# Fuse weights read from PSUM, low weights moved to GpSimd, and a new order in the tail of a transformer and convolution kernel

## What is computed

```
xn = layernorm(x);  x = x + window_attention(xn)        # 8x8 windows, 8 heads, relative bias
x  = x + gelu(layernorm(x) @ w_mlp1) @ w_mlp2           # hidden 256
h  = pw1_w x + pw1_b                                    # pointwise, 64 -> 64
scores = sigmoid(fc2(relu(fc1(mean(h)))));  mask = the top 32 channels of each image
h  = relu(h);  offsets = tanh(mean(h) @ off_w + off_b)  # (B, 3, 2)
for i, (ksz, base) in ((3, dw3), (5, dw5), (7, dw7)):
    w = base[:32] * (1 + sigmoid(offsets[:, i, 0])) + tanh(offsets[:, i, 1])   # per image
    y_i = depthwise_conv((h * mask)[:, :32], w)
out = pw_w[:, :96] @ concat(y_3, y_5, y_7) + pw_b + x
```

## Time and profile before

| what | us |
|---|---|
| median of 3 runs | 320.33 |
| lowest and highest of them | 318.23, 321.41 |
| the profiled execution's own time | 316.19 |
| its span, first to last instruction | 314.3 |
| busy: TensorE, weight loads | 269.3, 212.8 |
| busy: VectorE, ScalarE, GpSimd | 231.6, 204.7, 154.4 |
| mean granted TensorE clock | 0.965 |

### The profile page before, as it was taken

How to read it: one execution, slowest core, us unless ns; L and a number is a source line. 1 busy time by engine, 2 the same in 40 slices (tenths; PEclk the granted TensorE clock), 3 DMA queues, 4 the chain that set the end, 5 groups by cost and what they waited for, 6 DMA issues and landing times.

```text
span 314.3 us, 6646 instructions
## 1 busy us (share of the span) xinstructions
PE 269.3 (86%) x2486; PEld 212.8 (68%) x2486; DVE 231.6 (74%) x450; ACT 204.7 (65%) x331; POOL 154.4 (49%) x193
## 2 busy tenths in 40 slices
PE   1566869899999999999989799968995999799992
PEld 1334656777767677776868546644495999699992
DVE  2867527488787887878878554898799999998222
ACT  6686743858669595776745889976541764898800
POOL 5053444667678676875751707094577000444400
PEclk9996998999999999999989999997999799999998
DMA  7981357335334343443530000741306765699841
GB/s 163 200 170 46 76 129 159 82 84 111 88 81 98 85 86 73 100 103 74 114 93 3 2 0 2 161 95 28 89 12 121 154 148 103 151 185 190 180 80 33
DMA packets 35118, 31.06 MB, mean 99 GB/s; under 512 B 20816, under 2 KB 30032, under 8 KB 35088
## 3 DMA queue, kind: packets, MB, share of 16 engines
q1 hardware_dynamic: 30608, 23.55, 32.5%
q0 software_dynamic: 3392, 6.17, 11.2%
q10 hardware_dynamic: 1088, 0.94, 1.5%
HBM read 4.54 MB, written 2.10 MB: 21 GB/s over the span
## 4 chain that ended last, share of the span: by engine, by line
PE 34%; DVE 23%; POOL 19%; issue 11%; SPq 5%; ACT 4%; DMA 3%; DVEq 0%; POOLq 0%; ACTq 0%
PE psum L1256 11%; POOL parts L334 8%; PE psum L1001 5%; POOL k_blocks L551 5%; POOL q_blocks L559 4%; PE psum L1157 3%; SPq L446 3%; PE psum L922 2%; PE psum L1061 2%; DMA k_heads<-k_parts 2%; PE psum L1020 2%; PE psum L975 2%; DVE conv_w L334 2%; DVE whole_w L1624 2%; SPq L458 2%
## 5 line engine op out<-in xcount | busy, mean ns | idle before, releaser
L1256 PE MATMUL psum<-shifted,conv_w 128*128 128x286 f32 x528 | 73.2, 299 | 2.0 <-ACT conv_w L849 1.8
L1256 PEld LDWEIGHTS psum<-shifted,conv_w 128*128 128x128 f32 x528 | 71.3, 192 | 3.5 <-issue 3.5
L1001 PE MATMUL psum<-q_heads,k_blocks 128*128 128x256 f32 x384 | 63.3, 304 | 2.8 <-ACT probs L707 2.2
L1001 PEld LDWEIGHTS psum<-q_heads,k_blocks 128*128 128x128 f32 x384 | 52.4, 194 | 13.8 <-ACT probs L707 6.3
L1406 DVE TENSOR_REDUCE maxima<-psum 128x8 f32<-128x512 f32 x64 | 40.5, 680 | 7.2 <-PE psum L975 7.2
L707 ACT ACTIVATE probs<-psum 128x512 f32<-128x512 f32 x64 | 37.6, 605 | 11.6 <-PE psum L1001 10.5
L551 POOL DMA_DIRECT2D k_blocks<-k_parts x56 | 32.2, 582 | 8.6 <-PE psum L1001 8.6
L334 POOL TENSOR_TENSOR conv_w<-whole_w,conv_w 128x1408 fp32r<-128x1408 f32 x4 | 12.9, 3226 | 40.8 <-ACT conv_w L843 40.8
L334 POOL TENSOR_TENSOR parts<-x,parts 128x256 fp32r<-128x256 f32 (+1 forms) x21 | 19.3, 930 | 27.7 <-ACT parts L656 20.0
L922 PE MATMUL psum<-parts,center_average 128*128 128x512 f32 x64 | 23.9, 457 | 9.7 <-DVE parts L334 7.9
L334 POOL TENSOR_TENSOR parts<-square_logvar,parts 128x512 fp32r<-128x512 f32 x13 | 19.2, 1480 | 26.1 <-ACT square_logvar L720 15.8
(11 more groups left out here) (154 smaller groups left out, 509.9 us busy)
## 6 DMA issues: line engine op xcount, KB each, us to landing
shifted<-images SPq DMA_DIRECT2D x32, 243.8 KB, 4.5
q_heads<-q_parts SPq DMA_DIRECT2D x128, 32.0 KB, 2.3
k_blocks<-k_parts POOLq DMA_DIRECT2D x56, 64.0 KB
k_heads<-k_parts SPq DMA_DIRECT2D x64, 32.0 KB, 2.2
out<-x SPq DMA_DIRECT2D x8, 256.0 KB, 3.3
q_blocks<-q_parts POOLq DMA_DIRECT2D x28, 64.0 KB, 2.4
conv_w<-conv_w SPq DMA_DIRECT2D x10, 176.0 KB, 3.6
x<-in_x SPq DMA_DIRECT2D x6, 256.0 KB, 5.1
```

Source lines behind the costliest of these rows:

```text
L1001: ins = pe.matmul(bank[:, hh * G // 2:(hh + 1) * G // 2], k_blocks[:, hh, w // (NW // 2), k_part, w % (NW // 2), :], q_heads[:, w // (NW / ...
L1256: ins = pe.matmul(psum[:, CONV[bh][g], 0:SPAN], conv_w[bh][:, w_part, h * NSLOT + slot, :], shifted[:, bh, part, stream, first:first + SPA ...
```

## The change

- `fuse_w` is copied once into a PSUM bank (`fuse_bank`) between the high and low parts of the last group's second layer norm, and `factors` reads it from there for all units; `whole_weights_by_banks` is otherwise as it was.
- GpSimd computes the low weights of units 2 and 3 too; VectorE's `low_weights(1, 0)` and `(1, 1)` are gone. `whole_weights_by_banks` now always waits for the low weights of unit u - 2.
- All pointwise products from group 2 on use one bank and wait for the ReLU of the group before. The MLP's result goes to bank 7 for groups 3 to 6; two hidden blocks of group 1 use two banks freed by the layer norm. The order of the first MLP products changes.
- ScalarE: `gelu(7)` ahead of `even_high(0)`, `relu(7)` (the last) ahead of `even_high(1)`, and gate 2 behind all moves of unit 2's high part.
- TensorE: gate 1's steps and gate 2's `gate_means` and `gate_scores` stand later.
- VectorE: each `add_mlp` from 4 on stands one place earlier, `gate_means(2)` ahead of the products of unit 2, `gate_spread(2)` ahead of the additions of unit 3 but behind its products.

```diff
@@ -259,7 +259,7 @@
             "gate_dve", "gate_pe", "gate_act", "dv_product", "dv_whole", "po_no_row", "ac_high", "ac_odd", "ac_odd_high", "low_weights", "dv_odd",
             "shift_in0", "shift_in1", "pe_conv", "dv_result", "out_done")}
 
-        HIDDEN0, MLP, PW1, GATE = 3, 1, (7, 2), 0
+        HIDDEN0, MLP, PW1, GATE = 3, 1, 2, 0
         CONV = ((3, 4, 5), (2, 6, 7))
 
         def x_view(g, s):
@@ -292,12 +292,12 @@
         fuse_bank = psum[:, MLP, 320:512].rearrange("p (m c) -> p m c", c=C)
         product5_banks = psum[:, GATE:MLP + 1, 0:320].rearrange("p h (s c) -> p h s c", c=C)
 
-        def factors(b4, bh, m, fuse=fuse_w):
+        def factors(b4, bh, m):
 
             shape = [128, NKT // TAP, KERNELS[m], C]
             tap = tap_w[:, m, bass.ds(2 * b4 + bh, 1), :]
             tap = tap.rearrange("p b (h x) -> p (b h) x", x=TAP)[:, :, TAP - KERNELS[m]:]
-            return tap.unsqueeze(3).to_broadcast(shape), fuse[:, m, :].unsqueeze(1).unsqueeze(1).to_broadcast(shape)
+            return tap.unsqueeze(3).to_broadcast(shape), fuse_bank[:, m, :].unsqueeze(1).unsqueeze(1).to_broadcast(shape)
 
         ODD_ROWS = ((64, 0, 64, 0, 0, NTILE), (32, 64, 32, 0, 0, NTILE), (0, 96, 32, NSLOT, 0, NSLOT))
 
@@ -310,16 +310,19 @@
         MEANS = 48
 
         def pointwise_bank(n):
-            return GATE if n < 2 else PW1[1 - n % 2]
+            return GATE if n < 2 else PW1
+
+        def hidden_bank(n, m):
+            return (MLP, NORM)[m] if n == 1 and m < 2 else HIDDEN0 + m
 
         def norm2_bank(c):
             return PV if isinstance(c, int) and c == NG - 1 else NORM
 
         def means_bank(k):
-            return MLP if k == 2 else GATE
+            return PV if k == 2 else GATE
 
         def mlp_bank(n):
-            return MLP if n < NG - 1 else HIDDEN0 + 2
+            return MLP if n < 3 else PV if n < NG - 1 else HIDDEN0 + 2
 
         MAX_BANKS = (MAX0, MAX0 + 1, MISC1)
 
@@ -628,7 +631,7 @@
             for n in range(5, NG):
                 low_image(n, n // 2, n % 2)
 
-            for u in range(4, B):
+            for u in range(2, B):
                 bh = u % 2
                 pool.wait_ge(S["ac_high"], u + 1)
                 low_part(pool, whole_w[:, bh].rearrange("p h t c -> p (h t) c"), conv_w[bh][:, 0, :, 0:C], conv_w[bh][:, 1, :, 0:C]).then_inc(S["low_weights"], 1)
@@ -811,7 +814,7 @@
             def gelu(n, par, blocks=range(4)):
                 for m in blocks:
                     act.wait_ge(S["pe_mlp1"], 4 * n + m + 1)
-                    act.activation(hidden[:, par, m, :], psum[:, HIDDEN0 + m, :], ACT.Gelu,
+                    act.activation(hidden[:, par, m, :], psum[:, hidden_bank(n, m), :], ACT.Gelu,
                                    bias=mlp1_bias[:, m % 2:m % 2 + 1]).then_inc(S["ac_gelu"], 1)
 
             def relu(n, b4, half):
@@ -842,13 +845,12 @@
                     act.wait_ge(S["pe_conv"], u - 1)
                 act.copy(conv_w[bh][:, 0, :, 0:C], whole_w[:, bh].rearrange("p h t c -> p (h t) c")).then_inc(S["ac_high"], 1)
 
-            def odd_high(u, bh, moves=range(3), done=True):
+            def odd_high(u, bh, moves=range(3)):
                 act.wait_ge(S["ac_high"], u + 1)
                 for m in moves:
                     to, of = odd_rows(bh, 0, m)
                     ins = act.copy(to, of.bitcast(F32))
-                if done:
-                    ins.then_inc(S["ac_odd_high"], 1)
+                ins.then_inc(S["ac_odd_high"], 1)
 
             def odd_low(u, bh):
                 act.wait_ge(S["low_weights"], u + 1)
@@ -889,20 +891,19 @@
             relu(3, 1, 1)
             gelu(6, 0)
             relu(4, 2, 0)
+            gelu(7, 1)
             even_high(0, 0)
+            relu(5, 2, 1)
             odd_high(0, 0, range(1))
-            gelu(7, 1)
             gate(1)
-            relu(5, 2, 1)
             relu(6, 3, 0)
+            relu(7, 3, 1)
             even_high(1, 1)
             odd_high(1, 1, range(1))
-            relu(7, 3, 1)
             keep_shared(0, 0)
             even_high(2, 0)
-            odd_high(2, 0, range(1), done=False)
+            odd_high(2, 0)
             gate(2)
-            odd_high(2, 0, range(1, 3))
             odd_low(2, 0)
             keep_shared(1, 1)
             high_weights(3, 1)
@@ -1054,11 +1055,15 @@
                 pe.wait_ge(S["dv_normed2"], 2 * n + 2)
                 for m in blocks:
                     bh, f = m // 2, m % 2
-                    if n > 0:
+                    if n == 1 and m == 0:
+                        pe.wait_ge(S["ac_log2"], NG - 1)
+                    elif n == 1 and m == 1:
+                        pe.wait_ge(S["dv_whole2"], NG - 1)
+                    elif n > 0:
                         pe.wait_ge(S["ac_gelu"], 4 * n + m - 3)
 
                     for part in range(2):
-                        ins = pe.matmul(psum[:, HIDDEN0 + m, :], mlp1_w[:, part, f * 128:(f + 1) * 128],
+                        ins = pe.matmul(psum[:, hidden_bank(n, m), :], mlp1_w[:, part, f * 128:(f + 1) * 128],
                                         normed2[:, bh, bass.ds(n * G, G)], start=part == 0, stop=part == 1)
                     ins.then_inc(S["pe_mlp1"], 1)
 
@@ -1145,7 +1150,10 @@
 
 
             def mlp2(n, par):
-                pe.wait_ge(S["ac_log2"], NG - 1)
+                if n == 0:
+                    pe.wait_ge(S["ac_gelu"], 5)
+                if n == 3:
+                    pe.wait_ge(S["dv_whole2"], NG)
                 if n == NG - 1:
                     pe.wait_ge(S["ac_gelu"], 4 * NG)
                 elif n > 0:
@@ -1162,15 +1170,13 @@
 
                 pe.wait_ge(S["dv_x2"], n + 1)
                 if n == 0:
-                    pe.wait_ge(S["dv_whole2"], NG - 1)
+                    pe.wait_ge(S["ac_gelu"], 6)
                 if n == 1:
                     pe.wait_ge(S["ac_relu"], 1)
                 if n == 2:
                     pe.wait_ge(S["ac_log2"], NG)
-                if n == 3:
-                    pe.wait_ge(S["dv_whole2"], NG)
-                if n > 3:
-                    pe.wait_ge(S["ac_relu"], n - 1)
+                if n > 2:
+                    pe.wait_ge(S["ac_relu"], n)
                 pixels = x2[:, bass.ds(n * G, G)].rearrange("p (y v k q) -> p q v y k", v=2, q=2, k=W // 2)
                 for q in range(2):
                     ins = pe.matmul(psum[:, pointwise_bank(n), q * G // 2:(q + 1) * G // 2], pw1_w, pixels[:, q], start=True, stop=True)
@@ -1210,14 +1216,15 @@
                 pe.matmul(psum[:, GATE, 0:n], mem["score_rep"][0:n], consts[0:n, a:a + n], start=True, stop=True).then_inc(S["gate_pe"], 1)
 
             mlp1(0, range(2, 4))
+            mlp1(1, range(0, 2))
             projection(NG - 1)
-            mlp1(1, range(0, 2))
+            mlp1(1, range(2, 4))
             mlp2(0, 0)
-            mlp1(1, range(2, 4))
+            mlp1(2, range(0, 2))
             pointwise1(0, 0)
             centered2(NG - 1)
             mlp2(1, 1)
-            mlp1(2)
+            mlp1(2, range(2, 4))
             pointwise1(1, 1)
             variance2(NG - 1)
             mlp1(3)
@@ -1238,12 +1245,12 @@
             pointwise1(4, 0)
             mlp2(5, 1)
             mlp1(7)
-            gate_means(1)
             pointwise1(5, 1)
             mlp2(6, 0)
+            gate_means(1)
+            mlp2(7, 1)
             gate_scores(1)
             pointwise1(6, 0)
-            mlp2(7, 1)
 
 
             def passes(bh, w_part, g):
@@ -1297,13 +1304,13 @@
             low_passes(0, 0)
             high_weights_in(0, 1)
             passes(1, 0, 0)
+            passes(1, 0, 1)
             gate_means(2)
-            passes(1, 0, 1)
-            gate_scores(2)
             passes(1, 0, 2)
             low_passes(0, 1)
+            gate_scores(2)
+            high_passes(1, 0)
             gate_spread(2)
-            high_passes(1, 0)
             low_passes(1, 0)
             high_passes(1, 1)
             low_passes(1, 1)
@@ -1621,6 +1628,7 @@
 
 
             def products(b4, bh):
+                dve.wait_ge(S["dv_fuse"], 1)
                 dve.tensor_tensor(taps_window(whole_w[:, bh], 2), *factors(b4, bh, 2), ALU.mult)
                 dve.tensor_tensor(product5[:], *factors(b4, bh, 1), ALU.mult)
                 dve.tensor_tensor(product3[:], *factors(b4, bh, 0), ALU.mult).then_inc(S["dv_product"], 1)
@@ -1649,11 +1657,10 @@
 
             def whole_weights_by_banks(b4, bh):
                 u = 2 * b4 + bh
-                if u >= 6:
-                    dve.wait_ge(S["low_weights"], u - 1)
-                dve.tensor_tensor(product5_banks, *factors(b4, bh, 1, fuse_bank), ALU.mult)
-                dve.tensor_tensor(product3[:], *factors(b4, bh, 0, fuse_bank), ALU.mult)
-                dve.tensor_tensor(taps_window(whole_w[:, bh], 2), *factors(b4, bh, 2, fuse_bank), ALU.mult).then_inc(S["dv_product"], 1)
+                dve.wait_ge(S["low_weights"], u - 1)
```

(24 more changed lines are left out.)

## The result

The changed kernel took 317.64 us, the kernel before 319.92 us (medians of 20 runs each); the ratio is 0.991 with an interval of 0.988 to 0.994. It became faster by 0.9%, where 0.2% slower was forecast.

The account below looks back on a forecast made before the run. The start of unit 4, behind VectorE's queue, was taken to bound the kernel. Unit 4 0.9 us earlier, plus 1.5 us for the clock, made 0.6 us over before's median of 320.33: 320.9 us, range 316.3 to 324.3.

Parts of the forecast that it names:

- Part 1: Products of units 0 to 2 with fuse weights in PSUM: no turns with GpSimd, 4.4 us of VectorE time gained.
- Part 2: Low weights of units 2 and 3 on GpSimd: 3.2 us off VectorE, but a gate_mask(2) step waits 1.6 us.
- (b): TensorE's gate_scores(2) moved behind unit 1's low passes: VectorE waits for it, idle some 2.9 us.
- (d): Earlier add_mlp steps remove VectorE's idle 0.75 and 1.79 us; TensorE's 3.51 us stretch shrinks to about 1.
- Rival D: PSUM products still take turns with GpSimd, giving back about 2.5 us: 323.4 us; chance 0.03.
- the sum along the new chain: Step lengths laid out in the new order, from unit 0's products to unit 4's start at 272.6, 0.9 us earlier.
- nine steps ... add 5.4: Nine VectorE steps up to unit 1's whole weights may each wait for a GpSimd image piece, adding 5.4 us.
- rival B: Image pieces and unit 1's additions miss each other, unit 1's weights at 229 to 230: 315.9 us; chance 0.2.
- so I add 1.5 us at the start of unit 4: TensorE idles 3.7 us ahead of unit 4, so its clock falls and costs 1.5 us.

Follow-up runs that it names:

- e3: The changed kernel with TensorE's gate_means(2) and gate_scores(2) back inside unit 1's high passes; ratio to the kernel before 0.982, tail 129.3 us.
- e1: The changed kernel with the products of units 0 to 3 reading the fuse weights from SBUF again; ratio to the kernel before 1.000.
- e4: The changed kernel with the last ReLU behind unit 1's casts again; ratio to the kernel before 0.987, tail 133.3 us.
- e2: The changed kernel with the low weights of units 2 and 3 on VectorE again; ratio to the kernel before 0.988, tail 132.4 us.
- e13: The changed kernel with gate 2's scores early, the last ReLU late, gate_spread(1) later and gate_spread(2) earlier on TensorE; ratio to the kernel before 0.983.

## Why the prediction was wrong

**The mechanisms.** Most are in the trace. (A unit is one image; the prediction calls it a pair, and nothing hangs on that.) Part 1: clear products beside GpSimd; PSUM costs nothing. Part 2: 1.6 us in the mask step, as taken. (b): 3.11 us idle ahead of the scores, forecast 2.9. (d), the miss: TensorE's 3.51 us stretch is gone, but VectorE still idles 1.71 us at 212.56, where I had 0.6; unit 1's products start at 221.7 all the same (222.2 forecast), which is luck: those of unit 0 started 1.4 us ahead of the forecast (208.57, not 210.0), and that made up for it. The clock fell behind 3.53 us, forecast 3.7. e3 shows that the move of the scores costs what was said, and e1 that part 1 carries most of the gain. Rival D is out.

**First failed step, the sum along the new chain: "nine steps ... add 5.4".** They added 3.8: from 221.71, the start of unit 1's products (222.2 forecast), to 231.5 is 9.8 us, of which 6.0 are clear (2.3 + 1.1 + 2.6). Four of the nine waited 0.5 us or more, the longest 0.9, and two not at all. The weights of unit 1 came at 231.5 instead of 233.6. This is rival B by half. It did not come through one for one: the prediction had unit 1 wait for its weights, but TensorE came late from the slow clock that the 2.40 us at `gate_spread(1)` had brought, and set the start itself (e4, and the three profiles of the changed kernel). The prediction had an idle stretch only ahead of unit 1, and no fall of the clock there. Unit 4 started at 271.5, 1.1 us ahead of the forecast.

**Second failed step: "so I add 1.5 us at the start of unit 4" to the changed kernel alone.** The step set one profiled execution of before, in which the clock held at unit 4, against a kernel in which it falls every time. Before pays the same 1.5 us in two of four executions, and starts unit 4 up to 1.9 us later in them. This baseline was 1.4 us under the mean tail of its kernel (133.7 against 135.1).

Told in tails, the forecast was 0.6 us over the 133.7 of the first profile, 134.3. The changed kernel's mean is 132.6, so its sum was 1.7 us too long: on the mean of three profiles unit 4 starts 1.5 us ahead of the forecast, and the fall of the clock costs 1.3 instead of 1.5. The kernel before was taken 1.4 us too short. Together that turns 0.6 us slower into 2.5 us faster, where the medians have 2.3. That these agree so closely is partly luck, since single tails of one kernel lie up to 3.4 us apart.

The range held the time; the sign did not come out, since the forecast of 0.6 us is the difference of two sums, each off by 1.4 to 1.7 us.

## What to carry to other kernels

Where VectorE's two-SBUF-input steps and GpSimd's reading steps overlap, a factor that never changes belongs in PSUM; what is left (small gate steps, additions) waits if it is laid into GpSimd's busiest stretch, though taking it out pays only where its result is what the end waits for (e4: 1.7 us earlier weights, the same unit 4). Before a small matmul that the other engines wait for is moved behind a block of passes, count who is queued behind its result: here the change gave 0.9%, and 1.8% without this move. A forecast of under 1% needs several profiles of the kernel before; with one, the clock and the start of the tail are a draw.

## What the runs showed of the hardware that I had not expected

- Idle times of TensorE near 2 us are undecided, at the same place and in the same kernel too. The following matmuls ran at the full clock behind 1.79, 1.93, 2.02, 2.09, 2.25 and 2.32 us; they did not behind 1.93 and 2.00 us in two other executions (36.66 and 36.65 us for 264), nor behind 2.18 us in e2 and 2.25 in e13 (10.50 and 10.55 us for 66). Behind 2.03 us ahead of the last projection the clock held in four executions and fell in one; behind 2.40 us it mostly fell (6.0 to 7.1 us for 32) and once held (4.47). In these tails three or more us always brought the fall (3.09, 3.48 to 3.61, 3.95). What decides was not settled.
- The part ahead of the last projection comes in two lengths, in both kernels: of the seven profiles of the two, three have it at 180.2 to 180.6 us and four at 183.3 to 184.0. In the kernel before, the two with the later projection (183.3, 183.8) are the two in which the clock fell at unit 4; the changed kernel's have the shorter tails (132.1 and 132.2 against 133.3). What couples them was not tried.
